# An expert layer's loads: one train per landed scatter-add in place of each load when its buffer is free

## The reference

```
logits = x @ gate.T; the best 8 of 48 kept experts for each of the 4096 tokens
pos    = a token's place in its expert's list; places from 192 on are dropped
gu     = xb[e] @ gate_up[e].T          (192 rows x 384)
h      = silu(g) * u
out[e] = h @ down[e].T                 (192 rows x 512)
final[token] += out[e][pos] * weight   (a scatter-add over the tokens)
```

## Time and profile before

| what | value |
|---|---|
| median of 3 runs | 1284.0 us (1283.92 to 1286.0) |
| profiled execution | 1285.87 us |
| its span in the trace | 1284.1 us |
| expert stage: first row load issued to the end | 845.5 to 1284 us |
| TensorE busy | 1057.7 us, 82% of the span |
| DVE / ACT / POOL busy | 881.9 / 605.8 / 538.5 us |

### The profile page before, as it was taken

One profiled execution on the slowest core, in us unless ns is written; L12 is line 12 of the kernel. 1 busy time (PEld: TensorE's weight loads), 2 busy tenths in 40 slices (PEclk: granted clock), 3 DMA queues, 4 the chain that ended last, 5 costly groups with the idle time before them and its releaser, 6 DMA issues.

```text
span 1284.1 us, 24553 instructions
## 1 busy us (share of the span) xinstructions
PE 1057.7 (82%) x6474; PEld 851.7 (66%) x6474; DVE 881.9 (69%) x2462; ACT 605.8 (47%) x1703; POOL 538.5 (42%) x529
## 2 busy tenths in 40 slices
PE   6985898988888988898899897349888888889892
PEld 5773766766766766776677675248777777777682
DVE  5893776777777776777677775437767777777682
ACT  4542344344444443434444444136655666566561
POOL 2123554455455454454445555622332333333233
PEclk9997998899999998889899997669989999999997
DMA  8986335233222112111211211038989999999983
GB/s 304 341 287 243 141 140 179 105 143 139 83 65 80 44 41 75 48 41 41 82 41 41 74 33 39 12 117 252 259 232 256 229 238 253 242 266 247 257 214 49
DMA packets 80110, 191.80 MB, mean 149 GB/s; under 512 B 23175, under 2 KB 23175, under 8 KB 79568
## 3 DMA queue, kind: packets, MB, share of 16 engines
q1 hardware_dynamic: 44112, 130.70, 31.5%
q0 software_dynamic: 31344, 40.07, 14.8%
q10 hardware_dynamic: 4624, 20.68, 4.8%
HBM read 122.30 MB, written 121.87 MB: 190 GB/s over the span
## 4 chain that ended last, share of the span: by engine, by line
issue 37%; POOL 23%; DMA 23%; DVE 8%; PE 3%; POOLq 2%; ACT 1%; another core or an unknown queue 1%; DVEq 0%; SPq 0%; ACTq 0%
DMA layer_out<-qk_both,scatter_idx 20%; POOL slot_records L493 12%; POOL rstd L504 5%; POOL layer_out L539 3%; DVE qk_both L901 3%; DVE diff L896 2%; POOL qk_rot L517 2%; POOL rstd_h L521 1%; DMA slot_records<-row,slot_idx 1%; PE ps L1222 1%; DMA w_raw<-slot_records 1%; PE ps L1083 1%; PE ps L1068 0%; DMA w_raw<-in_weights 0%
## 5 line engine op out<-in xcount | busy, mean ns | idle before, releaser
L493 POOL DMA_INDIRECT slot_records<-row,slot_idx x256 | 257.2, 1005 | 93.1 <-issue 83.8
L539 POOL DMA_INDIRECT layer_out<-qk_both,scatter_idx x96 | 138.1, 1438 | 293.2 <-DVE scatter_idx L1002 224.9
L504 POOL TENSOR_TENSOR rstd<-mv,neg_half 128x1 f32<-128x1 f32 x96 | 79.6, 829 | 256.9 <-DVE mv L842 99.5
L553 ACT ACTIVATE xn_t<-ps 128x512 f32<-128x512 f32 x64 | 38.3, 599 | 177.1 <-PE ps L1068 146.6
L1083 PE MATMUL ps<-w_high,xn_high 128*128 128x512 f32 x384 | 113.4, 417 | 0.7 <-ACT xn_high L553 0.7
L1222 PE MATMUL ps<-w_high 128*128 128x192 f32 x576 | 92.9, 284 | 24.3 <-DVE w_low L988 23.7
L1083 PE MATMUL ps<-w_high,heads_high 128*128 128x512 f32 x128 | 50.1, 527 | 75.3 <-ACT heads_high L553 71.2
L1083 PE MATMUL ps<-w_high,xn_low 128*128 128x512 f32 x384 | 110.1, 409 | 0.0
L1083 PE MATMUL ps<-w_low,xn_high 128*128 128x512 f32 x384 | 108.3, 404 | 0.0
L1222 PEld LDWEIGHTS ps<-w_high 128*128 128x128 f32 x576 | 79.1, 197 | 40.9 <-issue 39.7
L592 ACT ACTIVATE probs<-ps,neg_max_s 128x128 f32<-128x128 f32 x256 | 90.0, 377 | 13.5 <-DVE neg_max_s L798 11.9
(11 more groups left out here) (164 smaller groups left out, 2613.7 us busy)
## 6 DMA issues: line engine op xcount, KB each, us to landing
gu_sb<-in_gate_up SPq DMA_DIRECT2D x48, 768.0 KB
dn_both<-in_down_proj SPq DMA_DIRECT2D x48, 512.0 KB
slot_records<-dn_both ACTq DMA_DIRECT2D x1, 20196.0 KB, 95.9
w_raw<-slot_records SPq DMA_DIRECT2D x48, 420.8 KB
x_ln<-in_x SPq DMA_DIRECT2D x32, 256.0 KB
x_res<-in_x SPq DMA_DIRECT2D x32, 256.0 KB
ctx_t_sb<-in_ctx_t SPq DMA_DIRECT2D x32, 256.0 KB
ctx_sb<-in_ctx_rows SPq DMA_DIRECT2D x32, 256.0 KB
```

The lines of the kernel that those rows point to most:

```text
L493: pool.indirect_dma_start(out=records, out_offset=bass.IndirectOffsetOnAxis(ap=slot_idx[:, s.parity, k:k + 1], axis=0), in_=row[:, s.parit ...
L504: pool.tensor_tensor(rstd[:, :], mv[:, 1:2], neg_half[:, 0:1], ALU.pow).then_inc(steps.sem, 1)
L539: pool.indirect_dma_start(out=out, out_offset=bass.IndirectOffsetOnAxis(ap=scatter_idx[:, d.parity, h:h + 1], axis=0), in_=y[:, d.parity, ...
L553: act.activation(dst, src, ACT.Copy).then_inc(steps.sem, 1)
```

## The change

Each expert's loads are issued together in the order gate_up(e+1), down(e), rows(e+1), after a new wait of SP: until the scatter-add of expert e-4 has landed. The waits for the free buffers stay. The first loads (gate_up and rows up to expert 4, down up to expert 3) have no such wait. In POOL's turn the four waits before the scatter-add are the same, in another order: the landing of the scatter-add before is waited for last.

```diff
+    def next(self):
+        return Batch(self.pair, self.off + 1, self.limit)
...
-                   nc.scalar.engine: sem("scalar_paced")}
+                   nc.scalar.engine: sem("scalar_paced"), nc.sync.engine: sem("sync_paced")}
...
             load_gate_up(Batch(1, 0, E))
-            with sp.Fori(1, E // 2 - 1) as pair:
+            load_rows(Batch(1, 0, E))
+
+            def load_for(e):
+                if e.back(4).exists():
+                    sp.wait_ge(d_add[e.parity], moved(e.back(4), 2))
+                    settled(sp)
+                if e.next().exists():
+                    load_gate_up(e.next())
+                load_down(e)
+                if e.next().exists():
+                    load_rows(e.next())
+            for off in range(2):
+                load_for(Batch(1, off, E))
+            with sp.Fori(2, E // 2 - 1) as pair:
                 for off in range(2):
-                    load_gate_up(Batch(pair, off + 1, E))
-                    load_rows(Batch(pair, off, E))
-                    load_down(Batch(pair, off, E))
-            load_gate_up(Batch(E // 2 - 1, 1, E))
+                    load_for(Batch(pair, off, E))
             for off in range(2):
-                load_rows(Batch(E // 2 - 1, off, E))
-                load_down(Batch(E // 2 - 1, off, E))
+                load_for(Batch(E // 2 - 1, off, E))
...
+                    pool.wait_ge(dwn_i.sem, dwn_i.after(d, "index"))
+                    pool.wait_ge(dwn_a.sem, dwn_a.after(d, "y0"))
+                    pool.wait_ge(dwn_v.sem, dwn_v.after(d, "y1"))
                     if d.back(1).exists():
                         pool.wait_ge(d_add[d.back(1).parity], moved(d.back(1), 2))
-                    pool.wait_ge(dwn_a.sem, dwn_a.after(d, "y0"))
-                    pool.wait_ge(dwn_v.sem, dwn_v.after(d, "y1"))
-                    pool.wait_ge(dwn_i.sem, dwn_i.after(d, "index"))
                     settled(pool)
```

## The result

| | before | changed |
|---|---|---|
| median of 4 runs each | 1284.35 us | 1341.24 us (1336.18 to 1349.45) |
| ratio, 95% interval | | 1.0447 [1.0391, 1.0503] |
| profiled execution, its span | 1285.87, 1284.1 us | 1343.45, 1341.7 us |
| first row load issued | 845.54 us | 848.76 us |
| period of the expert stage | 8.59 us | 9.93 us |

The changed kernel is slower by 57 us; 1330 had been forecast. The page of the changed kernel, part 2 (40 slices) and the shares by line of its chain: the DMA engines, at nine tenths in nearly the whole last third of the earlier trace rows, now stand at seven and eight.

What follows compares the result with a forecast made beforehand. DMA work and the scatter-add chain bound the kernel; queues empty at each landing make periods 9.7 us, not 8.59: 43 periods +48, head -2, tail 0, sum +46 on 1284.0, so 1330 us, range 1280 to 1356.

Steps and rivals of the forecast that it cites:

- Head: Before expert 1's scatter-add: gate_up for expert 5 now waits, so expert 0's scatter-add is freed of it; -2 us.
- Tail: From expert 44's scatter-add start to the span's end: no train before either, 0 us, bounds -1 and +2.
- (a): After a landing SP wakes, increments, does the next wait and issues gate_up: 0.3 us, bounds 0.2 and 0.6.
- (b): From gate_up's issue to its first packet: 0.9 us; down and rows follow under its transfer at no cost.
- (c): Transfer of the train of loads, 1.71 MB, each period: 5.41 us by its share, at least 4.7 us.
- (d): The scatter-add's packets, served behind the train: 2.64 us by their share, at least 2.2 us.
- (e): From the scatter-add's last packets to its landing: 0.65 us.
- I take 9.7 us, between the two: Period of the expert stage, chosen between the sum of 9.9 us and the second way's 9.5 us.
- The second way: Period from one observed 10.30 us landing to landing, less about 0.8 us for gate_up's later issue there: 9.5 us.
- Served behind the whole train: DMA queues: the scatter-add's packets move only after all the train's loads, even rows issued 1.5 us after its first half.
- POOL's order: POOL's reordered waits save 0.16 us a period, hidden under the train; without a train in front, up to 7 us.
- Levelling: Rival: queues share engines packet by packet, DMA never empty, period 8.0 us, 1257 us in all; chance 0.17.

Runs made afterwards that it cites:

- split train: Changed kernel, gate_up(e+2) issued after POOL issued the scatter-add of e-3, down and rows still waiting for the landing of e-4; 1.0261 of the kernel before, period 9.55 us.
- The run with the issue of e-3: Changed kernel, with expert e's loads waiting for POOL's issue of the scatter-add of e-3 instead of the landing of e-4; 1.0823 of the kernel before.

## Why the prediction was right

The forecast was slower by 46 us through queues that stand empty at each landing; measured were 57 us, by the same mechanism.

**The account.** 43 x (9.93 - 8.59) = 57.5 us. Head: from the first row load to expert 1's scatter-add 35.66 us before and 32.59 now, -3.1 us where -2 was taken (bounds 0 and -3). Tail: 33.60 and 33.58 us, 0 as taken. The first stage, which the change doesn't touch, ended 3.2 us later in this execution. Together 57.6 us, the difference of the spans (1341.7 - 1284.1).

**(a), (b): 0.3 + 0.9 us.** Right: gate_up 0.2 to 0.4 us after the landing, first data packet after 1.2 to 1.3 us.

**(c): 5.41 us.** Right, 5.39.

**(d), (e): 2.64 + 0.65 us.** The scatter-add's packets took 2.19 us, the lower bound, less than the mean of before. In its place the empty time was 2.34 us, not 0.3 + 0.9 + 0.65 = 1.85: 1.56 us without any packet, and 0.8 us in which the queues fill and drain. So DMA was busy 76%, not the 83% that was given as a sign. The two errors, -0.45 and +0.49, cancel, so the sum of 9.90 us met 9.93 partly by luck.

**The size.** Of the 11 us that the forecast missed (12 between the profiled executions), 10 are the step "I take 9.7 us, between the two" (43 x 0.23), 3 the later end of the first stage, and -1 the head. The second way, the observed 10.30 us less 0.8, was too low by 0.4 us; the sum alone would have given 1339 us.

**Order of service.** "Served behind the whole train" was half right. The changed trace repeats what the earlier trace rows showed: 285 packets of queue 1 and none of queue 0 from 1021.2 to 1025.7 us. Then both queues move side by side, 107 and 112 packets to 1028.2, so the sign "queue 0 packets only behind the train's" failed for half of them. The prediction's own stretch held the same. From 894.0 to 897.7 us queue 1 had more than is shown there, the train's last rows and then a down load that SP issued only at 894.09:

```profile
q1 hardware_dynamic: 179, 0.67, 47.0%
```

The sum doesn't hang on it, since both queues' work is paid before the landing in either order. What did carry the forecast is the late start of queue 0: its first packet came 4.4 to 5.4 us after POOL's first issue in the changed kernel, and 2.0 us after it where no load stood in front. So it ends last, and no load is left to fill the gap. The split train shows the limit: a load issued 1.8 us behind a scatter-add overtakes part of it. The turns between queues of which the Trainium skill tells (page "DMA: Bandwidth & Descriptors", section "Queues, rings and completion order") fit that stretch, with 134 and 69 packets side by side, and the one with 107 and 112; they don't fit the 4.5 us before it, unless queue 0 had nothing to serve yet, which no run here tells.

**POOL's order.** Hidden in the changed kernel, as said. The figure for a kernel without a train in front, up to 7 us of gain, had the wrong sign: alone it cost 7 to 11 us.

**The rivals.** Levelling did not happen under the gate, though the queues did share the engines for some 2.5 us of each period. Its price was near: without the wait the mean period was 8.2 to 8.3 us for 8.0, and the time fell by 1 to 2%. But the periods stayed uneven, so evenness was not what gave it. TensorE's clock did fall, from 0.96 to 0.91 of full, and its busy time rose from 7.57 to 8.16 us a period; it did not become the bound. SP's 43 waits for a landing exclude that the gate never binds.

**Late loads.** The prediction gave them no price below a period's slack. The run with the issue of e-3 puts the edge between the changed kernel's trains (0.2 to 0.4 us after the landing) and its own (4.4 to 11.1 us).

**Open.** What holds queue 0 back while a train is in front; why POOL's earlier issue widens the swing; why down, rows, gate_up in one train (10.31 us) has 0.23 us more of empty time and 0.14 us more of loads than gate_up, down, rows (9.93), with the same bytes.

## What to carry to other kernels

When a transfer engine is 90% busy, a gate that lets loads go only when the last transfer of the loop has landed caps what is out at one round; price it by the time from landing to the first packet plus the draining at the end, paid in every round, and look in the trace for a round in which the queues ran empty by chance, since it shows the changed kernel's period in advance. A gate one round earlier cost about 0.5% beside the same order without a gate. The new order of the loads alone gave 1 to 2%; that a load which the consumer in front waits for (rows here) belongs ahead of one that is needed later is the likely reason, not a shown one.

## What was not expected of the hardware

- The scatter-add's 224 packets take 2.19 us of all engines' time where half of them move beside the end of a train and the rest behind it, 2.63 us on average before, and 3.1 to 3.2 us in the changed kernel's last four periods, with one load or none beside them.
- A load issued 1.8 us after a scatter-add's second half moves among its packets and delays its landing to 7.09 us; with little or no load beside it, it is mostly 4.2 to 4.4 us (4.37 in the earlier trace rows), and 5.2 us for expert 45 in the changed kernel, with no load beside it.
- Halving the bytes of gate_up's load, at the same number of packets, saved 0.89 us of all engines' time; half of its bytes at the best rate in the earlier trace rows would be 1.1 us.
- The kernel before took 1243 to 1299 us from chip to chip; over all runs the first row load was issued between 797 and 856 us, while the expert stage's periods agree from chip to chip (8.23 and 8.32 us without the wait, 9.93 and 9.90 us with it).
